# A decoder layer on one core: the loops over the head groups written out on the four computing engines

## The reference

```
x = layernorm(x + gelu(x @ ((w1.T @ w2.T) * sparse_mask) + b2))
q = rope(x @ wq)          32 heads of 128
k, v = rope(ctx @ wk), ctx @ wv       8 heads of 128, each shared by 4 query heads
x = layernorm(x + softmax(q k / sqrt(128) + mask) v @ wo)
x = layernorm(x + x @ W.T + b + routed low-rank part (8 experts of rank 16))
```

## Time and profile before

| what | value |
|---|---|
| device time, median of 3 runs | 486.99 us (485.63 to 487.55) |
| device time of the profiled execution | 485.88 us |
| its span, first to last instruction | 484.0 us |
| PE busy | 470.2 us (97%) |
| DVE, ACT, POOL busy | 401.4, 268.7, 261.4 us |
| one steady pass of the loop | 46.79 us |

### The profile page before, as it was taken

The page is one execution under the profiler, slowest core; times in us unless marked ns, Lnnn a source line. Parts: engine busy times, 40 slices in busy tenths (PEclk is TensorE's granted clock), DMA queues, the critical chain, the costliest instruction groups (busy, mean ns, idle before and its releaser), DMA issues.

```text
span 484.0 us, 11244 instructions
## 1 busy us (share of the span) xinstructions
PE 470.2 (97%) x4289; PEld 389.8 (81%) x4289; DVE 401.4 (83%) x714; ACT 268.7 (56%) x466; POOL 261.4 (54%) x256
## 2 busy tenths in 40 slices
PE   8999999999999999999999999999999999999994
PEld 7878887878888888888888888888888888777773
DVE  2678788888889888888798888888888889999576
ACT  4572647836383648364835574466546544585344
POOL 3387646955395549455935693467357444155300
PEclk9999999999999999999999999999999999999998
DMA  8954100240023002400240022013002400000004
GB/s 285 340 168 166 45 1 1 88 131 2 1 87 130 0 0 87 130 0 0 87 129 0 13 105 99 0 56 111 6 0 87 69 2 1 2 0 1 1 1 174
DMA packets 29137, 31.56 MB, mean 65 GB/s; under 512 B 6321, under 2 KB 16817, under 8 KB 29114
## 3 DMA queue, kind: packets, MB, share of 16 engines
q1 hardware_dynamic: 29114, 31.25, 20.3%
HBM read 29.15 MB, written 2.10 MB: 65 GB/s over the span
## 4 chain that ended last, share of the span: by engine, by line
PE 81%; DVE 10%; SPq 4%; issue 2%; DMA 1%; ACT 1%; POOL 1%; ACTq 0%; POOLq 0%
PE bank L272 24%; PE bank L273 23%; PE bank L274 23%; PE bank L380 7%; SPq L216 2%; DVE BST L1227 2%; PE bank L389 2%; DMA WQr<-in_L_xattn_wq_dram 1%; DVE VWl L1179 1%; DVE X L1374 1%; DVE X L1431 1%; PE bank L278 1%; DVE NW L1268 1%; DVE XTl L1179 1%; DVE NW L1270 1%
## 5 line engine op out<-in xcount | busy, mean ns | idle before, releaser
L1760 POOL TENSOR_TENSOR QS<-QS,SIN 128x512 f32<-128x512 f32 x64 | 82.9, 1296 | 114.0 <-ACT QS L814 113.6
L272 PE MATMUL bank<-XTh,WQh 128*128 128x512 f32 x256 | 100.9, 394 | 0.0
L1179 DVE TENSOR_TENSOR VWl<-bank,VWh 64x512 fp32r<-64x512 f32 x128 | 88.0, 687 | 14.8 <-ACT VWh L814 13.1
L273 PE MATMUL bank<-XTl,WQh 128*128 128x512 f32 x256 | 99.8, 390 | 0.0
L274 PE MATMUL bank<-XTh,WQl 128*128 128x512 f32 x256 | 99.8, 390 | 0.0
L814 ACT ACTIVATE VWh<-bank 64x512 fp32r<-64x512 f32 x128 | 75.8, 592 | 24.9 <-PE bank L274 22.5
L814 ACT ACTIVATE QS<-bank 128x512 f32<-128x512 f32 x64 | 38.3, 598 | 70.1 <-PE bank L274 70.0
L272 PEld LDWEIGHTS bank<-XTh,WQh 128*128 128x128 f32 x256 | 48.1, 188 | 10.4 <-DVE QR L1319 0.2
L274 PEld LDWEIGHTS bank<-XTh,WQl 128*128 128x128 f32 x256 | 48.1, 188 | 10.2
L1307 DVE TENSOR_TENSOR bank<-bank,COS 128x512 f32<-128x512 f32 x64 | 44.6, 697 | 13.8 <-ACT QS L814 12.8
L273 PEld LDWEIGHTS bank<-XTl,WQh 128*128 128x128 f32 x256 | 48.1, 188 | 9.7 <-issue 0.2
(11 more groups left out here) (159 smaller groups left out, 942.4 us busy)
## 6 DMA issues: line engine op xcount, KB each, us to landing
WQr<-in_L_xattn_wq_dram SPq DMA_DIRECT2D x8, 1024.0 KB, 5.5
WOr<-in_L_xattn_wo_dram SPq DMA_DIRECT2D x8, 1024.0 KB, 5.4
KVr<-in_L_xattn_wk_dram SPq DMA_DIRECT2D x8, 256.0 KB, 5.0
KVr<-in_L_xattn_wv_dram SPq DMA_DIRECT2D x8, 256.0 KB, 5.2
out_dram<-X SPq DMA_DIRECT2D x8, 256.0 KB, 2.0
X<-in_x_dram SPq DMA_DIRECT2D x3, 512.0 KB, 10.3
WQr<-in_L_attn_w_dram SPq DMA_DIRECT2D x4, 256.0 KB, 4.7
WOr<-in_L_attn_w_dram SPq DMA_DIRECT2D x4, 256.0 KB, 5.7
```

Source lines behind the costliest of these rows:

```text
L272: pe.matmul(o, lh, rh, start=start, stop=False)
L273: pe.matmul(o, lh, rl, start=False, stop=False)
L1179: return dve.tensor_tensor(o, i, f32(hi), ALU.subtract)
L1760: pool.tensor_tensor(q, q, SIN[:, :].unsqueeze(1).broadcast_to([P, 2, S]), ALU.mult)\
```

## The change

In four places a hardware loop becomes a loop of the Python program, which writes its body six times with g = 1 to 6. Nothing else is touched; SP keeps its loop.

```
-            with pe.Fori(1, LAST) as g:
+            for g in range(1, LAST):
                 pe.wait_ge(sm["k_cos"], g + 1)
                 query(g, 0, 0)
...
-            with act.Fori(1, LAST) as g:
+            for g in range(1, LAST):
                 q_copy(g, 0, 0)
...
-            with dve.Fori(1, LAST) as g:
+            for g in range(1, LAST):
                 q_cos(g, 0, 0)
...
-            with pool.Fori(1, LAST) as g:
+            for g in range(1, LAST):
                 q_sin(g, 0, 0)
```

## The result

The changed kernel takes 487.17 us (median of 12 runs, 486.45 to 487.74), the kernel before 486.16 us on the same chip (median of 12, 485.5 to 487.55). The ratio is 1.0018, 95% interval 1.001 to 1.0026: +0.88 us, between +0.5 and +1.3. It is slower by 0.2%, inside the 0.5% that count as no change here, and 0.8 us under the forecast time.

What follows compares the result with a forecast made beforehand. PE's bare matmul stream was taken to bound the kernel, apart from instruction-fetch holes. Holes of 2.3 us against 1.3 before gave +1.0 us on the 486.99 us median, so 488.0 us, range 485.0 to 491.5.

Steps and rivals of the forecast that it cites:

- rule for where a border hurts: At PE's `score_pair` bursts: a 256-instruction block border costs time only from about -5 to 42 instructions behind a pair's start.
- Branches and register waits on PE are worth 0: PE's loop: removing jumps and register arithmetic gains 0, since the sequencer handles them ahead of PE.
- The rival in which the loop stood in PE's way: PE's loop: jumps and register waits cause the 0.35 us idles at small tiles; -4.2 us, 482.8 us, chance of faster 0.06.
- The other engines are worth 0: ACT, DVE and POOL: dropping their register arithmetic and fetching their longer programs change the time by 0.
- 34 packets, 0.56 MB: Queue 8, carrying PE's program: 34 packets, give or take one, and about 0.56 MB, where there were 15 packets.
- A cold pass is free but for its holes: The six passes on PE: stretches from pair to pair stay 46.8 us long except where a hole falls.
- The rival in which each pass pays 0.98 us: Later five passes: each costs what the first did, +4.9 us, 491.9 us; chance 0.16 for wholly or more than half.
- Distance 7, 0.5 us: First pair of the first pass, border 7 instructions behind its start: a hole of 0.4 to 0.6 us, taken as 0.5.
- Distance 1, 0.75 us: Second pair of the fifth pass, border 1 instruction behind its start: a hole of about 0.75 us near 304 us.
- Distance -4, 1.05 us: First pair of the sixth pass, border 4 instructions ahead of its start: a hole of 1.05 us near 330 us.
- Before, 1.3 us: Kernel before, its three cold pairs with borders at -2, 42 and 30: holes of 1.06, 0.11 and 0.17 us, together 1.3.
- The sum, +1.0 us: Whole kernel: holes of 2.3 us after the change against 1.3 us before, so +1.0 us.

Runs made afterwards that it cites:

- the padding: 66 semaphore increments that nobody waits for, added on PE ahead of the loop to the changed kernel; 487.95 us, ratio 1.0032 [1.002, 1.0044] to the kernel before.

## Why the prediction came out right

Its mechanism held: the block borders of PE's program cost the time. Its rule for where a border hurts failed at one of three places. Step by step:

- *Branches and register waits on PE are worth 0.* Held. Stretches without a hole are 46.78 us in both kernels, and the idle of 0.35 us stands 13 times in both. The rival in which the loop stood in PE's way is out: five jumps cost nothing, and PE's program written out takes 1.0022 [1.001, 1.0035] of the time before. The Trainium skill (Runtime: NRT & Kernel Launch, Instruction fetch mechanics) says that a taken branch forces a fetch where its target lies outside a window of two pages, and by that rule the prediction priced a fetch at each jump; on PE, with a body of this size, no run here shows one. The same section gives PE 128 KiB for instructions, and with that figure the trace agrees, for the body's 62 KB fit in it.
- *The other engines are worth 0.* Held: 0.9997 [0.9988, 1.0006].
- *34 packets, 0.56 MB.* Held to the packet, so the counting of PE's instructions was right.
- *A cold pass is free but for its holes.* Held. Passes two to four and six are cold and as long as warm ones. The rival in which each pass pays 0.98 us is out. (The 0.98 was itself a little short: the stretch in the earlier trace rows begins at 95.04 us, the scores at 94.96. The first pass took 142.81 - 94.96 - 46.79 = 1.06 us more, exactly its one hole.)
- *Distance 7, 0.5 us.* Right place, too small: it cost 0.97, and 1.03 with PE alone written out. The packet there took 1.33 us, and by the prediction's own working the next block was ready some 3.7 us after the border (3.25 + 0.97 - 0.5). Distance 12 costs 1.06, 17 0.68, 22 0.79. My 3.2 to 3.3 us came from two pairs that had lost little, where the packets took 0.88 and 0.93 us. How long the packet takes counts: with the same PE program and the border at 30, a packet of 0.93 us went with a loss of 0.17 us and one of 1.22 us with 0.38.
- *Distance 1, 0.75 us.* It cost 0.91, 0.16 more than the term. PE began this pair 0.6 us behind the sequencer's signal, not 0.3 as in before.
- *Distance -4, 1.05 us.* Failed: it cost nothing. I took it for the same case as the -2 of before, whose one packet in the stretch from 95 us on began 1.0 us after PE had started the pair. At -4 the packet had begun 1.4 us before PE's start of the pair. It lies within 329 to 331 us, ahead of the small matmuls at 331.71 and their transposes, where queue 8 shows:

```profile
q8 instruction: 1, 0.02, 3.2%
```

- *Before, 1.3 us.* Too much: 0.11 and 0.17 us of it cost the kernel nothing, as shown above, and 1.06 is left.
- *The sum, +1.0 us.* The terms come to 0.97 + 0.91 + 0 = 1.88 instead of 2.3, and before's to 1.06 instead of 1.3, so the holes give +0.82 us and the measurement +0.88 (0.5 to 1.3). That the sum came out so near is in part luck: three errors nearly cancel, +0.6 us at distances 7 and 1, -1.05 at -4 and +0.3 in before's share.
- *The time, 488.0 us.* I added to the median of three runs, 486.99; beside the changed kernel before had 486.16. That is 0.8 us, as much as the change itself.

What all the holes have in common is when the fetch starts. In the 18 holes of 0.1 us or more inside the scores the packet starts 1.0 to 1.7 us after the sequencer's signal `s_begun` of that pair, wherever the border lies from -16 to 30, and PE goes on 1.2 to 1.6 us after the packet's end, 3.4 to 3.8 us after the signal (packet starts and lengths as the traces hold them; at distance 7 the signal ends at 94.64, the packet lasts from 95.77 to 97.10, and PE goes on at 98.44). So "the next block is ready 3.2 to 3.3 us after the border" was not the right rule: it was ready 3.4 to 3.8 us after the signal, and what a hole costs depends on how early PE gets through the 256 instructions.

What the runs do not settle is where the window opens. The cold pairs near a border, loss in us in the pair or right behind it, by distance of the border; the pair behind the loop counts with the first pairs:

| first pairs | -22, -21, -10, -5, -4 | -2 | 1 | 7 | 10 | 12 | 27 | 30 | 39 |
|---|---|---|---|---|---|---|---|---|---|
| loss | 0 | 1.06 | 0.67 | 0.97 | 0.48 | 1.06 | 0.11 | 0.17 | 0 |

| second pairs | -38 | -16 | -5 | 0 | 1 | 6 | 17 | 22 | 39 | 42 |
|---|---|---|---|---|---|---|---|---|---|---|
| loss | 0 | 0.68 | 0.98 | 0.54 | 0.91 | 0.92 | 0.68 | 0.79 | 0.14 | 0 |

From 44 on it is 0 in both, and it is large from 0 to 22. The border at 30 behind the loop cost 0.38 us in the run with PE's program unchanged, so a single entry is good to about 0.2 us. Below 0 the two kinds differ, -16 costs in a second pair and -4 does not in a first, and the difference goes with when the packet starts: 0.5 us after the second pair has begun, 1.4 to 3.9 us before the first where its border is at -4 to -10. In both kinds the sequencer stands for about 3 us in the wait for `q_rot` ahead of the pair (L395, with the padding L399). With the border at -4 in a first pair, then with -16 in a second (duration in ns, start in us):

```profile
L395 PEldq EVENT_SEMAPHORE  x1: 3261/3261/3261, 327.1 to 327.1; - x1
L399 PEldq EVENT_SEMAPHORE  x1: 2932/2932/2932, 348.3 to 348.3; - x1
```

The first of the two packets starts within this wait, at 329.6 us; the second only at 352.7, 1.5 us behind its end. Why the second isn't fetched during the wait as well remains open. So does why some packets begin several us after their border.

## What to carry to other kernels

In this kernel a loop whose body stays beside the engine (999 instructions of PE) was fetched once, and its jump cost nothing while the sequencer ran ahead. Writing it out made every pass cold, and that cost time only where a border of PE's 256-instruction blocks fell into a burst of small matmuls. Before such an edit, or any that adds instructions ahead of a burst, count PE's instructions to the burst: moving a border by three took 0.9 us (0.2%) off this kernel, as much as lies between its two ways of writing the loop. A difference of 0.2% between two versions of one kernel may be nothing but this count.

## What the hardware showed that I had not expected

- PE kept the whole body of its loop. From the second pass on it fetched nothing for the rest of the loop, though the body is 999 of its instructions, 62 KB in four packets of 16 KB.
- The packets of the two queues differ in size: 0.56 MB in 34 on PE's queue, 16 KB each, and 0.11 MB in 13 on the other, some 8 KB each.
- A semaphore increment that stands alone takes 0.15 us of PE's sequencer (18 of them made the first matmul 2.0 us late), and costs little or nothing where PE has work in its queue (with 80 of them the ratio is still 0.9986 [0.9975, 0.9998]).
- PE can use up 256 instructions faster than the next 256 arrive: a pair puts 288 through in 2.67 us. At the holes the packet alone took 0.9 to 1.3 us, began 1.0 to 1.7 us after the sequencer had come to the pair, and PE went on 1.2 to 1.6 us after its end.
- A stall of PE isn't always a loss: 0.17 us behind the loop vanished in a wait for DVE that shrank from 0.46 to 0.29 us.
